# Router logits by token from the turned tile, twenty row homes, loops that skip an empty turn

## The chip, the core and the metric

The kernel runs on one core of a Trainium2 chip. The metric is device time in microseconds of one execution. The core has five engines that run their own instruction streams and meet at semaphores: TensorE (PE in the profile), VectorE (DVE), ScalarE (ACT), GpSimd (POOL) and SyncE (SP), which here only issues transfers. Before the change three runs took 599.23, 604.85 and 601.07 us, median 601.07.

## The reference, cut to what matters

There are 4 x 1024 = 4096 tokens of width H = 1024, a context of width D = 256, and E = 8 experts.

```python
def _L0_xattn_ref(x, adj, W, b):          # x is the context, adj the normed input
    si = jnp.einsum('bnd,d->bn', x, Wi[0])
    sj = jnp.einsum('bnd,d->bn', x, Wj[0])
    xij = jax.nn.sigmoid(si[:, :, None] + sj[:, None, :] + b[0])
    return P_ASEM * xij + (1.0 - P_ASEM) * adj

def _L0_ffn_ref(x, wg, W, b):
    xt = x.reshape(-1, Hv)
    logits = xt @ wg                       # 4096 x 8
    probs = jax.nn.softmax(logits, axis=-1)
    idx = jnp.argmax(probs, axis=-1)
    ...                                    # only the chosen expert's gate is kept
    expert_out = jnp.einsum('nh,eoh->neo', xt, W) + b[None, :, :]
    return jnp.einsum('ne,neo->no', combine, expert_out)

x = x + jnp.tanh(g_xattn[0]) * _L0_xattn_ref(ctx_512, _layernorm(x), ...)
x = x + jnp.tanh(g_ffn[0]) * _L0_ffn_ref(_layernorm(x), ...)
```

## The kernel before, in words

**First stage: 32 tiles of 128 tokens.** A tile is loaded into one of RX = 16 homes of the tile `xr` (SP, L366). DVE takes its statistics six tiles ahead (`stats`, L836), ACT computes the tanh form of the sigmoid three tiles ahead (`half_tanh`, L645), POOL applies the norm two tiles ahead (`linear`, L507), and DVE adds the two (`add_tanh`, L847). PE turns the tile with eight transposes (`turn_tile`, L1134), ACT copies the turned tile out of PSUM (`copy_turned`, L661), and PE multiplies it by the router weights `wg` (`route`, L1146). `route(t - 1)` stands behind `turn_tile(t)` in PE's stream. In `route` the eight columns of `wg` are loaded as weights and the 128 tokens of the turned tile stream, so the logits come out expert by token (8 x 128). In float32 each of the eight matmuls over k is two passes in the trace, 16 in all.

**By token.** For every group of four tiles ACT copies the logits out of PSUM (`logits_copy`, L668), and PE turns them with four small matmuls (`logits_by_token`, L1158). Then DVE picks the expert (`choose`, L857 and following), PE counts ranks (`rank`, L1167 to L1173), DVE makes positions (`position`, L885 and L887), and POOL scatters the finished rows into a table in memory (`store`, L515), sorted by expert. A home is free for the next load when its row is stored. SP issues its loads in order; the load of tile 19 stands behind `spread_scores(2)` and that of tile 26 behind `spread_scores(3)`, which wait for scores of the context.

**Context.** Eight groups of context are turned (L1108, eight transposes) and summed with two columns (`sum_columns`, L1124): there each 128 x 128 block is loaded as weights and two columns stream, 16 passes for a group. Groups 0 to 3 come ahead of tile 0, groups 4 to 7 behind tiles 2, 6, 10 and 14.

**Second stage: slots.** The sorted rows are worked in slots of 128 rows of one expert. A slot is 48 matmuls of 128 x 512 on PE (L1213, three products of high and low parts). DVE and ACT turn and split rows (L907, L679, L912) and, in two slots of each expert, four pieces of the next weights (L894, L673, L899). POOL makes the gate from the row's scalars (`slot_scalars`, L542 to L556), adds the scaled bias (L559, from ACT's L743) and stores the sums (`store_sums`, L563). DVE's `finish` (L924) adds the product and frees PE's PSUM pair: slot t + 2 of PE waits for `finish` of slot t.

**The loops.** The number of slots is known only at run time. There is room for SLOTS = 48, in loops of 6 slots to a turn (SP: 2). Two slots are worked ahead of the loop. The loops of PE, DVE, ACT and SP load a number from `slot_tab` for every slot, and branch around the slot if it is empty. POOL's loop looks at the first slot of a turn and leaves out the whole turn if that is empty.

Of the kernel before, what the change touches and what calls it, by code (L numbers as in the profile page):

```python
# [7 lines left out]
P = 128  # L8
# [13 lines left out]
def build(nc, x, ctx, g_xattn, g_ffn, mix_w, mix_b, wg, W, bias, out):  # L22
# [15 lines left out]
    RX = 16  # L38
# [36 lines left out]
    with st:  # L75
# [20 lines left out]
        wj_bc = sb("wj_bc", [P, DC, P])  # L96
# [48 lines left out]
        with zone:  # L145
            xr = [sb("xr0", [P, GR, ROW], F32, zone)]
            sb("even_weights", [P, 2, K, H], F32, zone)
            th = sb("th", [P, RTH, H], F32, zone)
            xr.append(sb("xr1", [P, RX - GR, ROW], F32, zone))
            ctx_in = sb("ctx_in", [P, 2, GR * D], F32, zone)  # L150
            ctx_tr = sb("ctx_tr", [P, GR, DC, P], F32, zone)
            sj = sb("sj", [P, 2, P, TB], F32, zone)
            xc_tr = sb("xc_tr", [P, 2, K, P], F32, zone)
            told = sb("told", [P, H], F32, zone)


# [15 lines left out]
        sb("gap", [P, 2 * K * H + RTH * H + (RX - GR) * ROW - 4 * K * H])  # L172
# [10 lines left out]
        early_ps = small[:, 128:129]  # L183
        tot_ps = pair[3][:, 0:E]

        lgt = bias_bc[0:E, 1, 0:HALF].rearrange("e (r n) -> e r n", r=GR)
# [43 lines left out]
        lgt_copied = sem("lgt_copied")  # L230
        by_token = sem("by_token")
# [46 lines left out]
        def rows_at(s, n):  # L278
            return xr[0][:, s:s + n, :] if s < GR else xr[1][:, s - GR:s - GR + n, :]
# [31 lines left out]
        def _(sp):  # L311
# [28 lines left out]
            for t in range(12, RX):  # L340
# [19 lines left out]
            for t in range(RX, T):  # L360
# [4 lines left out]
                sp.wait_ge(row_stored[slot_of(t)], 16)  # L365
# [15 lines left out]
            for s in range(RX):  # L381
                sp.wait_ge(row_stored[s], 16 * (T // RX))
# [15 lines left out]
            sp.wait_ge(by_token, NG)  # L398
# [3 lines left out]
            with sp.Fori(0, SLOTS // 2) as i:  # L402
                for r in range(2):
                    t = 2 * i + r + AHEAD
                    work = sp.value_load(slot_tab[0:1, 0, bass.ds(t, 1)], min_val=0, max_val=3)
                    with sp.If(work > 0):
                        sp.wait_ge(xb_turned, t + 2)
                        load_blocks(sp, sp.value_load(slot_tab[0:1, 2, bass.ds(t + 3, 1)], min_val=0,
                                                      max_val=E * N - P), r + 3)
                        with sp.If(work > 1):  # L410

                            n = sp.value_load(slot_tab[0:1, 3, bass.ds(t, 1)], min_val=2, max_val=HALVES - 1)
                            with sp.If(n < HALVES - 1):
                                n = sp.value_load(slot_tab[0:1, 3, bass.ds(t, 1)], min_val=2, max_val=HALVES - 2)
                                for m in range(WR):
                                    sp.wait_ge(w_turned, WR * n + m + 1)
                                    load_piece_of(n + 1, m)
                            with sp.Else():
                                sp.nop()
                            with sp.If(work < 3):  # L420

                                e = sp.value_load(slot_tab[0:1, 1, bass.ds(t, 1)], min_val=0, max_val=E - 2)
                                sp.wait_ge(w_ready, K * e + K + 1)
                                sp.dma_start(bias_bc[:, bass.ds((e + 1) % 2, 1), :].rearrange("p a h -> p (a h)"),
                                             bias[bass.ds(e + 1, 1), :].to_broadcast([P, H])).then_inc(bias_landed, 16)
                            with sp.Else():
                                sp.nop()
                            sp.nop()
                        with sp.Else():
                            sp.nop()  # L430
                        sp.nop()
                    with sp.Else():
                        sp.nop()

        @block.gpsimd
        def _(pool):
# [13 lines left out]
            nc.gpsimd.memset(xr[0][:, :, VAR + 1:LG], 0.0)  # L450
            nc.gpsimd.memset(xr[1][:, :, VAR + 1:LG], 0.0)
# [87 lines left out]
            def slot_scalars(u, n, k, k2):  # L539
# [17 lines left out]
                    gate_ready, 1)  # L557
                settled(rb_ready, u + 1)
# [10 lines left out]
            slot_scalars(0, 0, 0, 0)  # L569
            pool.wait_ge(limits_told, 1)  # L570
            slot_scalars(1, 0, 1, 1)
            store_sums(0, 0)
            slot_scalars(2, 1, 2, 0)
            store_sums(1, 1)
            pool.wait_ge(slots_told, 1)

            def slot(t, r, i):
# [3 lines left out]
                store_sums(t, r)  # L581

# [15 lines left out]
            held = [pool.value_load(in_place[0:1, s:s + 1], min_val=E, max_val=SLOTS) for s in range(2)]  # L598
            filled = pool.value_load(n_filled[0:1, 0:1], min_val=2 * E, max_val=SLOTS)
# [670 lines left out]
```

## Time and profile before

| what | value |
|---|---|
| median of three runs | 601.07 us |
| the profiled execution | 600.74 us, its span 599.0 us |
| mean granted TensorE clock | 0.949 of full |
| PE matmul busy | 545.9 us, 91% |
| DVE busy | 403.8 us, 67% |
| POOL busy | 332.5 us, 56% |
| ACT busy | 279.6 us, 47% |

Times in the profile count from the start of the span. The first stage runs from about 22 us (first `add_tanh`) to 161.6 us (last `route`), the second from there to the last sum at 585.6 us. The granted clock is a share of full speed: 1.00 is 2.4 GHz and 0.50 is 1.2 GHz. A busy time of PE says that matmuls were in flight, not that they went at full speed.

### The profile page before, as it was taken

To read this page: it belongs to the slowest core of one execution; us is meant where nothing else is said; L and a number is where in the kernel's file an instruction comes from. 1 tells how busy PE (TensorE), PEld (TensorE's weight loads), DVE (VectorE), ACT (ScalarE), POOL (GpSimd) and SP (SyncE) were. 2 spreads that over 40 slices of the span, in tenths; PEclk is the share of its full clock that TensorE was granted. 3 is DMA by queue.
4 is the path that set the end of the run, shared out by engine and by line. 5 is a ranking of instruction groups with operands and counts; after the bars stand their busy time and mean duration, and the time that the engine had idled before them with its cause. 6 is when DMAs were issued, how large, how long until landed. Compare 5 with 4: busy or idle time off the path is not lost.

```text
span 599.0 us, 13888 instructions
## 1 busy us (share of the span) xinstructions
PE 545.9 (91%) x2818; PEld 443.0 (74%) x2819; DVE 403.8 (67%) x534; ACT 279.6 (47%) x408; POOL 332.5 (56%) x500
## 2 busy tenths in 40 slices
PE   8899988898898969799989999998998999999990
PEld 6787766666677848688868888877887888888880
DVE  2867777796889876956955794784588559834320
ACT  4698868789513424424432442443244244332220
POOL 1788888888344443364356436435544663466650
PEclk9699889889899979989989999999999999999996
DMA  8997677887967987976875787688568757554530
GB/s 273 361 292 236 200 277 258 293 286 233 330 219 211 273 244 210 271 236 187 258 238 179 209 253 252 192 242 243 181 193 263 235 178 212 173 178 152 181 124 6
DMA packets 84398, 135.23 MB, mean 226 GB/s; under 512 B 12048, under 2 KB 64784, under 8 KB 84368
## 3 DMA queue, kind: packets, MB, share of 16 engines
q1 hardware_dynamic: 68432, 81.88, 46.9%
q0 software_dynamic: 9792, 33.82, 14.5%
q10 hardware_dynamic: 6144, 19.18, 10.3%
q8 instruction: 13, 0.21, 0.1%
q14 instruction: 17, 0.14, 0.1%
HBM read 101.01 MB, written 35.93 MB: 229 GB/s over the span
## 4 chain that ended last, share of the span: by engine, by line
PE 27%; DVE 22%; issue 15%; DMA 13%; POOL 8%; ACT 5%; ACTq 4%; DVEq 2%; POOLq 1%; SPq 0%
PE pair L1213 21%; DMA rows<-table 7%; DVE wt L899 7%; DVE pair L894 4%; DMA table<-xr,pos 3%; PE pair L1146 3%; DVE xt L912 2%; ACTq L747 2%; PE pair L1134 2%; DVE xr L847 2%; DVE raw L836 2%; DMA gates<-in_L_xattn_b 2%; DMA xr<-in_x 2%; POOL scal L552 1%; ACT wt L673 1%
## 5 line engine op out<-in xcount | busy, mean ns | idle before, releaser
L1213 PE MATMUL pair<-wt,xt 128*128 (+1 forms) x1728 | 401.9, 394 | 19.7 <-DVE rows L924 16.7
L1213 PEld LDWEIGHTS pair<-wt,xt 128*128 128x128 f32 x1728 | 328.1, 190 | 92.5 <-issue 22.4
L559 POOL TENSOR_TENSOR rows<-rows,rb 128x1024 f32<-128x1024 f32 x37 | 88.9, 2401 | 64.6 <-ACT rb L743 64.6
L673 ACT ACTIVATE wt<-pair 128x1024 f32 (+1 forms) x64 | 65.6, 1027 | 69.0 <-DVE pair L894 68.9
L912 DVE TENSOR_TENSOR xt<-pair,xt 128x1024 fp32r<-128x1024 f32 x38 | 46.5, 1224 | 70.6 <-ACT xt L679 70.6
L894 DVE STREAM_TRANSPOSE pair<-w_raw 128x1024 f32<-128x1024 f32 x64 | 79.8, 1249 | 1.4
L899 DVE TENSOR_TENSOR wt<-pair,wt 128x1024 f32 (+1 forms) x64 | 77.2, 1207 | 3.7 <-ACT wt L673 3.7
L743 ACT ACTIVATE rb<-bias_bc,scal 128x1024 f32 (+1 forms) x37 | 46.0, 1245 | 66.2 <-POOL scal L556 66.2
L1146 PE MATMUL pair<-xc_tr,wg_sb 128*8 128x128 f32 x512 | 70.2, 298 | 0.0
L552 POOL TENSOR_TENSOR scal<-scal,minus_one 128x1 f32<-128x1 f32 x37 | 20.4, 551 | 83.4 <-ACT ez L735 83.4
L679 ACT ACTIVATE xt<-pair 128x1024 fp32r<-128x1024 f32 x38 | 39.1, 1028 | 59.1 <-DVE pair L907 38.5
L924 DVE SCALAR_TENSOR_TENSOR rows<-pair,scal,rows 128x1024 f32<-128x1024 f32 x36 | 46.1, 1281 | 28.9 <-PE pair L1213 28.9
L907 DVE STREAM_TRANSPOSE pair<-xb 128x1024 f32<-128x1024 f32 x38 | 47.8, 1258 | 21.9 <-DMA xb<-table 17.1
L1146 PEld LDWEIGHTS pair<-xc_tr,wg_sb 128*8 128x8 f32 x512 | 47.1, 97 | 16.4 <-issue 2.8
L1134 PE MATMUL pair<-ident,xr 128*128 128x128 f32 x256 | 37.9, 295 | 14.9 <-DVE xr L847 14.9
L515 POOL DMA_INDIRECT table<-xr,pos x32 | 37.1, 1158 | 22.6 <-DVE pos L887 12.8
L836 DVE BATCH_NORM_STATS2 raw<-xr 128x6 f32<-128x512 f32 x64 | 40.7, 677 | 11.8 <-DMA xr<-in_x 11.8
L1134 PEld LDWEIGHTS pair<-ident,xr 128*128 128x128 f32 x256 | 30.4, 152 | 22.3 <-DVE xr L847 18.5
L507 POOL TENSOR_SCALAR xr<-xr,ln_a,ln_b 128x1024 f32<-128x1024 f32 x32 | 43.7, 1366 | 3.2
L563 POOL DMA_INDIRECT out_x<-rows,scatter_row x36 | 38.6, 1073 | 11.5 <-issue 6.6
L735 ACT ACTIVATE ez<-rows,scal 128x8 f32<-128x8 f32 x37 | 11.0, 296 | 72.3 <-POOL scal L547 72.3
L847 DVE SCALAR_TENSOR_TENSOR xr<-th,c,xr 128x1024 f32<-128x1024 f32 x32 | 41.5, 1297 | 4.1 <-POOL xr L507 3.8
(138 smaller groups left out, 378.7 us busy)
## 6 DMA issues: line engine op xcount, KB each, us to landing
w_raw<-in_L_ffn_W SPq DMA_DIRECT2D x256, 128.0 KB, 3.0
xb<-table SPq DMA_DIRECT2D x156, 128.0 KB, 3.2
rows<-table ACTq DMA_DIRECT2D x36, 520.0 KB
xr<-in_x SPq DMA_DIRECT2D x32, 512.0 KB, 6.0
ctx_in<-in_ctx SPq DMA_DIRECT2D x8, 512.0 KB, 7.8
bias_bc<-in_L_ffn_b SPq DMA_DIRECT2D x8, 512.0 KB, 4.4
sj<-sj_row SPq DMA_DIRECT2D x3, 512.0 KB, 5.1
rows<-table SPq DMA_DIRECT2D x2, 520.0 KB
```

The source lines that it names most:

```text
L559: nc.gpsimd.tensor_tensor(rows[:, k, 0:H], rows[:, k, 0:H], rb[:, :], ALU.add).then_inc(base_ready, 1)
L673: nc.scalar.activation(wt[:, bass.ds(place, 1), 0, :, P * m:P * (m + 1)].rearrange("p a k o -> p (a k) o"), ps[:, :].rearrange("p (k o) -> ...
L836: last = nc.vector.bn_stats(raw[:, t % 2, h, :], row_at(s)[:, HALF * h:HALF * (h + 1)])
L847: nc.vector.scalar_tensor_tensor(out=row_at(s)[:, 0:H], in0=th[:, t % RTH, :], scalar=c2[:, 0:1], in1=row_at(s)[:, 0:H], op0=ALU.mult, op1 ...
L894: nc.vector.transpose(turned(ps), blocked(w_raw[:, m, :, :])).then_inc(w_turned, 1)
L899: nc.vector.tensor_tensor(where[:, :, 1].rearrange("p a k o -> p (a k) o"), ps[:, :].rearrange("p (k o) -> p k o", k=K), where[:, :, 0].re ...
L907: nc.vector.transpose(turned(ps), blocked(xb[:, k, :, :])).then_inc(xb_turned, 1)
L912: nc.vector.tensor_tensor(where[:, :, 1].rearrange("p a k n -> p (a k n)"), ps[:, :], where[:, :, 0].rearrange("p a k n -> p (a k n)").bit ...
L924: nc.vector.scalar_tensor_tensor(out=row_of, in0=out_ps[r % 2][:, :], scalar=scal[:, bass.ds(k, 1), 7:8].rearrange("p a b -> p (a b)"), in ...
L1134: last = nc.tensor.transpose(xt_ps[t % 2][:, P * k:P * (k + 1)], row_at(slot_of(t))[:, P * k:P * (k + 1)], ident[:, :])
L1146: last = nc.tensor.matmul(lgt_ps[:, r, :], wg_sb[:, k, :], xc_tr[:, t % 2, k, :], start=(k == 0), stop=(k == K - 1))
L1213: last = nc.tensor.matmul(out_ps[r % 2][:, HALF * h:HALF * (h + 1)], xt[:, r % RING, x_part, k, :], wt[:, bass.ds(place + h, 1), w_part, k ...
```

## The change

1. **Router.** In `route` the turned tile is loaded as weights, 128 columns, and the eight columns of `wg` stream. The logits come out token by expert at once, so `logits_copy` on ACT and `logits_by_token` on PE are gone (8 of each), and `choose` waits for `route` alone. Logits and ranks have two homes in PSUM, by turns.
2. **Homes.** RX is 20. Four homes lie where the second weight half will be, so ACT waits for the rows of homes 16 to 19 to be stored before it writes piece (1, 0), at tile 28.
3. **Loops.** PE, DVE, ACT and SP leave a turn if its first slot is empty, as POOL does. POOL's three loads of end counts stand ahead of its loop.
4. **Orders.** In a slot POOL stores the sums of slot t before it adds the bias of slot t + 1, and ACT issues the load of the rows of slot t + 2 before the scaled bias of slot t + 1.

```diff
-    RX = 16
+    RX = 20
...
-            xr = [sb("xr0", [P, GR, ROW], F32, zone)]
-            sb("even_weights", [P, 2, K, H], F32, zone)
...
+            xr_late = sb("xr_late", [P, GR, ROW], F32, zone)
+            sb("first_half", [P, 2, K, HALF], F32, zone)
+            xr_last = sb("xr_last", [P, GR, ROW], F32, zone)
+            sb("second_half", [P, 2 * K * HALF - GR * ROW], F32, zone)
...
-            xr.append(sb("xr1", [P, RX - GR, ROW], F32, zone))
+            xr_first = sb("xr_first", [P, RX - 2 * GR, ROW], F32, zone)
...
-        lgt_ps, small = pair[3][0:E, 0:HALF].rearrange("e (r n) -> e r n", r=GR), pair[3][:, HALF:2 * HALF]
-        lg_ps = small[:, 0:GR * E].rearrange("p (r e) -> p r e", e=E)
-        rank_ps = small[:, 64:64 + GR * E].rearrange("p (r e) -> p r e", e=E)
...
+        lg_ps = [pair[3][:, HALF * j:HALF * j + GR * E].rearrange("p (r e) -> p r e", e=E) for j in range(2)]
+        rank_ps = [pair[3][:, HALF * j + 64:HALF * j + 64 + GR * E].rearrange("p (r e) -> p r e", e=E) for j in range(2)]
...
+            for t in range(12, 16):
...
+            for t in range(16, T):
                 if t == 19:
                     spread_scores(2)
                 if t == 26:
                     spread_scores(3)
-                sp.wait_ge(row_stored[slot_of(t)], 16)
+                if t >= RX:
+                    sp.wait_ge(row_stored[slot_of(t)], 16)
                 sp.dma_start(row_at(slot_of(t))[:, 0:H], tile_of(x_t, t)).then_inc(x_landed[slot_of(t)], 16)
...
-            sp.wait_ge(by_token, NG)
...
+            with sp.Fori(0, SLOTS // 2) as i:
+                t = 2 * i + AHEAD
+                first = work_of(t)
+                with sp.If(first > 0):
+                    slot(t, 0, first)
+                    second = work_of(t + 1)
+                    with sp.If(second > 0):
+                        slot(t + 1, 1, second)
...
+            def add_base(u, k):
                 settled(rb_ready, u + 1)
                 nc.gpsimd.tensor_tensor(rows[:, k, 0:H], rows[:, k, 0:H], rb[:, :], ALU.add).then_inc(base_ready, 1)
...
+            held = [pool.value_load(in_place[0:1, s:s + 1], min_val=E, max_val=SLOTS) for s in range(2)]
+            filled = pool.value_load(n_filled[0:1, 0:1], min_val=2 * E, max_val=SLOTS)
...
             def slot(t, r, i):
                 slot_scalars(t + 1, RING * i + (r + 1) // 2, (r + 1) % RING, (r + 1) % 2)
                 settled(out_stored[r % 2], 16 * RING * i + 16 * (r // 2))
                 store_sums(t, r)
+                add_base(t + 1, (r + 1) % RING)
...
-            held = [pool.value_load(in_place[0:1, s:s + 1], min_val=E, max_val=SLOTS) for s in range(2)]
-            filled = pool.value_load(n_filled[0:1, 0:1], min_val=2 * E, max_val=SLOTS)
...
-            def logits_copy(g):
-                act.wait_ge(routed, GR * (g + 1))
-                if g:
-                    act.wait_ge(by_token, g)
-                nc.scalar.activation(lgt, lgt_ps, ACT.Copy).then_inc(lgt_copied, 1)
...
-                if r == 1 and g > 0:
-                    logits_copy(g - 1)
...
+                    if PIECE_AT[t] == (1, 0):
+                        for s in range(RX - GR, RX):
+                            act.wait_ge(row_stored[s], stores_from(s))
...
+            def slot(t, r, i, work):
+                behind = (r + 2) % RING
+                settled(summed, t + 1)
+                xt_high(t + 2, behind, cut_a)
+                with act.If(work > 1):
+                    n = table_of(3, t, HALVES - 1)
+                    home = act.snap(n % 4)
+                    for m in range(WR):
+                        cut_high(n, m, home, (cut_b, cut_a)[m % 2])
+                with act.Else():
+                    act.nop()
+                after = (r + 1) % RING
+                exp_sum(t + 1, after)
+                settled(out_stored[(r - 1) % 2], 16 * RING * i + 16 * ((r - 1) // 2) + 16)
+                load_rows(act, table_of(2, t + 2, E * N - P), r, behind)
+                e1 = table_of(1, t + 1, E - 1)
+                scaled_bias(t + 1, after, e1, act.snap(e1 % 2))
             with act.Fori(0, SLOTS // TURN) as i:
...
                 g, r = t // GR, t % GR
                 if t == 0:
                     pe.wait_ge(ctx_copied, GR)
-                if r == 0 and g > 0:
-                    pe.wait_ge(lgt_copied, g)
+                    pe.wait_ge(sj_col_ready, 2)
+                    pe.wait_ge(si_ready, GR)
+                if r == 0 and g > 1:
+                    pe.wait_ge(pos_ready, g - 1)
                 for k in range(K):
-                    last = nc.tensor.matmul(lgt_ps[:, r, :], wg_sb[:, k, :], xc_tr[:, t % 2, k, :],
+                    last = nc.tensor.matmul(lg_ps[g % 2][:, r, :], xc_tr[:, t % 2, k, :], wg_sb[:, k, :],
                                             start=(k == 0), stop=(k == K - 1))
                 last.then_inc(routed, 1)
...
-            def logits_by_token(g):
-                pe.wait_ge(lgt_copied, g + 1)
-                if g:
-                    pe.wait_ge(pos_ready, g)
-                else:
-                    pe.wait_ge(sj_col_ready, 2)
-                    pe.wait_ge(si_ready, GR)
-                for r in range(GR):
-                    last = nc.tensor.matmul(lg_ps[:, r, :], lgt[:, r, :], ident[0:E, 0:E], start=True, stop=True)
-                last.then_inc(by_token, 1)
...
                     pe.wait_ge(ahead_told, 1)
-                nc.tensor.matmul(rank_ps, ones_bf[:, :],
+                nc.tensor.matmul(rank_ps[g % 2], ones_bf[:, :],
...
-                if r == 1 and g > 0:
-                    logits_by_token(g - 1)
                 if r == 2 and g > 0:
                     rank(g - 1)
...
             with pe.Fori(0, SLOTS // TURN) as i:
-                for r in range(AHEAD, TURN + AHEAD):
-                    t = TURN * i + r
-                    work = pe.value_load(slot_tab[0:1, 0, bass.ds(t, 1)], min_val=0, max_val=3)
-                    with pe.If(work > 0):
-                        e = pe.value_load(slot_tab[0:1, 1, bass.ds(t, 1)], min_val=0, max_val=E - 1)
-                        multiply(t, r, e, pe.snap(2 * (e % 2)))
-                    with pe.Else():
-                        pe.nop()
+                with pe.If(work_of(TURN * i + AHEAD) > 0):
+                    slot(TURN * i + AHEAD, AHEAD)
+                    for r in range(AHEAD + 1, TURN + AHEAD):
+                        with pe.If(work_of(TURN * i + r) > 0):
+                            slot(TURN * i + r, r)
```

PE's stream at tiles 4 to 6 of the first stage, before (`xc_tr` is the turned tile, `wg_sb` the router weights, `bias_bc` the copied logits; names on the right of the arrow are what is read):

```order
L1134 MATMUL pair<-ident,xr 128x128 x8
L1158 MATMUL pair<-ident,bias_bc 128x8 x4
L1146 MATMUL pair<-xc_tr,wg_sb 8x128 x8
L1134 MATMUL pair<-ident,xr 128x128 x8
L1167 MATMUL pair<-cum,ones_bf 128x32
L1170 MATMUL pair<-onehot,ones_bf 128x24
L1170 MATMUL pair<-onehot,ones_bf 128x16
L1170 MATMUL pair<-onehot,ones_bf 128x8
L1173 MATMUL pair<-onehot,lower_bf 128x32
L1146 MATMUL pair<-xc_tr,wg_sb 8x128 x8
```

And of the change, at the same place:

```order
L1163 MATMUL pair<-ident,xr_first 128x128 x8
L1177 MATMUL pair<-wg_sb,xc_tr 128x8 x8
L1163 MATMUL pair<-ident,xr_first 128x128 x8
L1187 MATMUL pair<-cum,ones_bf 128x32
L1190 MATMUL pair<-onehot,ones_bf 128x24
L1190 MATMUL pair<-onehot,ones_bf 128x16
L1190 MATMUL pair<-onehot,ones_bf 128x8
L1193 MATMUL pair<-onehot,lower_bf 128x32
L1177 MATMUL pair<-wg_sb,xc_tr 128x8 x8
```

The four small matmuls are gone, and each router matmul gives 128 x 8 instead of 8 x 128: 8 columns stream where 128 did.

ACT's stream at the end of a slot in the loop, before (`ez` is the row's exponentials, `rb` the scaled bias):

```order
L735 ACTIVATE ez<-rows,scal 128x8
...
L743 ACTIVATE rb<-bias_bc,scal 128x1024
L611 ISA
L747 ISA
L747 TENSOR_LOAD slot_tab
L747 ISA x2
L307 ISA
L307 DMA rows<-table 128x1040
```

And of the change:

```order
L312 DMA rows<-table 128x1040
L761 ISA
L761 TENSOR_LOAD slot_tab
L761 ISA x2
L631 ISA
L757 ISA
L757 ACTIVATE rb<-bias_bc,scal 128x1024
L814 UNCONDITIONAL_BRANCH
```

The load of rows stood behind the scaled bias and now stands ahead of it.

## Rows read from the trace of the kernel before

**Rows 1.** The profile's page, its head and its row of granted clock, 40 slices.

```profile
span 599.0 us, 13888 instructions
...
PEclk9699889889899979989989999999999999999996
```

**Rows 2.** Busy time by stretch: length, each engine's busy time, clock, DMA share, GB/s.

```profile
22.00:157.00 135.00, 119.14 (x919) 92.96 (x918) 102.14 (x197) 108.93 (x179) 112.29 (x131) 0.89 0.80 267
217.00:584.00 367.00, 355.76 (x1536) 291.93 (x1534) 237.50 (x227) 135.28 (x180) 186.96 (x298) 0.98 0.69 211
```

**Rows 3.** Groups by line: busy us, mean ns, then idle before.

```profile
L1146 PE MATMUL pair<-xc_tr,wg_sb 128*8 128x128 f32 x512 | 70.2, 298 | 0.0
...
L1158 PE MATMUL pair<-ident,bias_bc 8*128 8x8 f32 x64 | 8.4, 254 | 1.0 <-ACT bias_bc L668 1.0
```

**Rows 4.** Timeline of PE, first stage: start, length, line, shape, count, idle before.

```profile
30.63 1.09 PE L1134 MATMUL pair<-ident,xr 128*128 128x128 f32 x8
31.65 1.91 PE L1146 MATMUL pair<-xc_tr,wg_sb 128*8 128x128 f32 x16
...
59.82 3.40 PE L1146 MATMUL pair<-xc_tr,wg_sb 128*8 128x128 f32 x16
...
152.12 1.97 PE L1134 MATMUL pair<-ident,xr 128*128 128x128 f32 x8 [1.33 <-DVE xr L847]
```

**Rows 5.** Timeline of PE from 13 to 22 us, the context ahead of tile 0.

```profile
13.42 1.93 PE L1124 MATMUL pair<-wcol,xc_tr 128*128 128x2 f32 x16
15.21 3.23 PE L1108 MATMUL pair<-ident,ctx_in 128*128 128x128 f32 x16
18.24 2.25 PE L1124 MATMUL pair<-wcol,ctx_tr 128*128 128x2 f32 x16
20.35 1.93 PE L1124 MATMUL pair<-wcol,xc_tr 128*128 128x2 f32 x16
```

**Rows 6.** PE by stretch: length, busy, granted clock, DMA share, GB/s.

```profile
16.00:18.00 2.00, 2.00 (x11) 0.50 1.02 399
20.00:22.00 2.00, 2.00 (x20) 1.00 1.00 401
22.00:24.00 2.00, 0.46 (x4) 0.62 1.01 414
```

**Rows 7.** Waits of DVE from 22 to 157 us: total, times, longest.

```profile
DVE top L857 <- PE pair L1158: 12.2, 5, 3.9
DVE raw L836 <- DMA xr<-in_x: 11.6, 4, 4.8
```

**Rows 8.** Waits over the whole span: total, times, longest.

```profile
PE pair L1213 <- DVE rows L924: 16.7, 6, 5.6
...
ACT xt L679 <- issue: 19.1, 16, 1.5
```

**Rows 9.** Timeline from 224 to 255 us, slots with weights.

```profile
224.98 1.24 ACT L743 ACTIVATE rb<-bias_bc,scal 128x1024 f32 x1 [1.82 <-POOL scal L556]
225.90 0.34 ACTq L307 DMA_DIRECT2D rows<-table  x1
227.35 1.03 ACT L679 ACTIVATE xt<-pair 128x1024 fp32r<-128x1024 f32 x1 [1.12 <-issue]
228.41 1.23 DVE L912 TENSOR_TENSOR xt<-pair,xt 128x1024 fp32r<-128x1024 f32 x1 [4.04 <-ACT xt L679]
...
254.93 5.35 PE L1213 MATMUL pair<-wt,xt 128*128 x16 [3.04 <-DVE rows L924]
```

**Rows 10.** Timeline of the end: the last sum and the last store.

```profile
584.33 1.28 DVE L924 SCALAR_TENSOR_TENSOR rows<-pair,scal,rows 128x1024 f32<-128x1024 f32 x1 [5.97 <-PE pair L1213]
...
586.51 1.07 POOL L563 DMA_INDIRECT out_x<-rows,scatter_row  x1 [2.44 <-DVE rows L924]
```

**Rows 11.** SP's waits, its last one in the span.

```profile
SPq L75 <- PEq L75: 15.0, 1, 15.0
```

**Rows 12.** DMA issues of the stores: count, median us to landing.

```profile
out_x<-rows,scatter_row POOLq DMA_INDIRECT x36, 4.3
```

More of the change, by code:

```diff
@@ L787, in _ @@
+            with act.Fori(0, SLOTS // TURN) as i:
+                first = table_of(0, TURN * i + AHEAD, 3)
+                with act.If(first > 0):
+                    slot(TURN * i + AHEAD, AHEAD, i, first)
+                    for r in range(AHEAD + 1, TURN + AHEAD):
+                        work = table_of(0, TURN * i + r, 3)
+                        with act.If(work > 0):
+                            slot(TURN * i + r, r, i, work)
                         with act.Else():
                             act.nop()
-                        after = (r + 1) % RING
@@ new lines, in slot @@
+            def slot(t, r, i, work):
+                behind, mine = (r + 2) % RING, r % RING
+                dve.wait_ge(xt_ready, t + 2)
+                turn_rows(t + 2, RING * i + r // 2 + 1, r % 2, cut_a)
+                with dve.If(work > 1):
+                    n = dve.value_load(slot_tab[0:1, 3, bass.ds(t, 1)], min_val=0, max_val=HALVES - 1)
+                    home = dve.snap(n % 4)
+                    for m in range(WR):
+                        turn_weights(n, m, (cut_b, cut_a)[m % 2])
+                        if m == 0:
+                            xt_low(t + 2, behind, cut_a)
+                            dve.wait_ge(xt_ready, t + 3)
+                        else:
+                            cut_low(n, m - 1, home, (cut_b, cut_a)[(m - 1) % 2])
+                    cut_low(n, WR - 1, home, cut_a)
+                    settled(w_ready, WR * n + WR)
+                with dve.Else():
+                    xt_low(t + 2, behind, cut_a)
+                finish(t, r, mine)
@@ new lines, in work_of @@
+            def work_of(t):
+                return dve.value_load(slot_tab[0:1, 0, bass.ds(t, 1)], min_val=0, max_val=3)
+            with dve.Fori(0, SLOTS // TURN) as i:
+                first = work_of(TURN * i + AHEAD)
+                with dve.If(first > 0):
+                    slot(TURN * i + AHEAD, AHEAD, i, first)
+                    for r in range(AHEAD + 1, TURN + AHEAD):
+                        work = work_of(TURN * i + r)
+                        with dve.If(work > 0):
+                            slot(TURN * i + r, r, i, work)
@@ L1084, in _ @@
                         with dve.Else():
-                            xt_low(t + 2, behind, cut_a)
-                        finish(t, r, mine)
-                    with dve.Else():
-                        dve.nop()
+                            dve.nop()
+                    dve.nop()
+                with dve.Else():
+                    dve.nop()
         @block.tensor
```

151 lines of the change are left out of this document (62 added, 89 removed).

## The prediction

> **What bounds the kernel now.** I began with the head of the page: a span of 599.0 us, and a row of granted clock that stands at 9 or 8 in most slices of the second half and dips to 7 in the first [rows 1]. The profiled execution took 600.74 us, so 1.7 us lie outside its span, and it is 0.3 below the median of 601.07; the sum below starts from 600.7. The busy time by stretch [rows 2] gives two stages with different limits. In the second stage, 217 to 584 us, PE is in flight for 355.8 of 367.0 us and its clock is 0.98: the stage is the matmuls plus the gaps between them. In the first, 22 to 157 us, no engine is full, but four are near it: PE 119.1 of 135.0 us, POOL 112.3, ACT 108.9, DVE 102.1, at a mean clock of 0.89. With 32 tiles from about 24 us to 161.6 us this is 4.3 us for a tile. Last I read the waits: DVE waits 12.2 us for the logits by token and 11.6 us for rows of x [rows 7], and PE waits 16.7 us for `finish` of two slots before, six times [rows 8].
>
> **The router, in columns.** Now 512 router passes take 70.2 us of PE and the 64 small passes 8.4 us [rows 3]. At full clock one tile is a turn of 1.09 us and a route of 1.91 us [rows 4]. Sixteen passes in which 128 x 128 blocks are the weights and two columns stream, the sums of the context, take 1.93 us at full clock [rows 5]. So to stream 8 columns in place of 128 gives nothing directly: the weight load sets the pace of such a pass, 1.91 against 1.93. What goes is the small matmuls, 8 x 1.05 us on PE, and eight copies of the logits on ACT.
>
> **The router, in clock.** This is where I expect the change to decide. Ahead of tile 0 PE does the same kind of work that the new `route` does, and the granted clock tells what it does to it. After the sums at 13.42 us the clock is 0.50 from 16 to 18 us, with PE in flight for 2.00 of 2.00 us [rows 6]; the transposes at 15.21 us, 128 streaming columns each, run at this level, 3.23 us for 16 [rows 5]. After them it is 1.00 from 20 to 22 us. The two groups of sums at 18.24 and 20.35 us follow without a break, and from 22 us it is 0.62, that is, it falls to 0.50 in the stretch [rows 6]. So passes with few streaming columns do not hold 2.4 GHz, however closely they stand, and passes with 128 columns bring it back. In the first stage today the route streams 128 columns in two thirds of PE's passes. After the change those have 8, and only the turn, 8 of 24 passes of a tile, streams 128.
>
> The Trainium skill ("TensorE: Matmul & The Clock Gate", Part 1, What's actually happening) says that activity releases the throttle and idle time restores it. If being in flight were that activity, the clock would stay up, and the time would be that of rival B; the trace speaks against it with 0.50 at 2.00 of 2.00 us.
>
> At the low clock a turn is 1.97 us and a route 3.40 us [rows 4]. The route of 3.40 us is the old form; I take the same for the new one, since both forms agree at full clock. A tile is then 1.97 + 3.40 less 0.15 for the overlap of the groups (31.72 against 31.65 us at full clock, twice that at the low one), 5.2 us. That is more than the 4.3 us of today, so PE becomes the bound of the stage, and neither DVE's waits nor POOL matter in it. The sum: 32 x 5.2 = 166.4 us; four groups of context behind tiles 2, 6, 10 and 14, each a turn and a set of 16 sums, 4 x 5.3 = 21.2 us; ranks some 2 us. From 24 us this ends at 213.6 us. Against it stand spells of high clock: where the 8 transposes of a context group stand beside the 8 of a turn there are 16 in a row, as at 15.21 us, and the spell that followed there began in the sums at 18.24 us and was over early in 22 to 24 us: a bit over 3 us in which PE does twice the work. Not each of the four will line up so well; I take three, worth 10 us. The last route then ends at 203.6 us instead of 161.6: **+42 us**. Bounds: +52 with no spell; +13 if the clock is low in only half of the tiles (16 x 5.2 + 16 x 4.3 + 8 for the sums of context at low clock = 160, from 24 to 184, less 10).
>
> The same skill page (Part 4, PE-mode transpose) says that a transpose does not count as PE being busy in the same way, so that full clock is not granted for it. By this there would be no spells, the stage would be longer, and the time that of rival D. The trace disagrees: the clock rose behind the 16 transposes of 15.21 us. It saw this once, though, and with matmuls of two columns ahead and behind.
>
> **The homes.** Rows of x come too late by 11.6 us in four waits [rows 7], as SP waits for the store of the tile 16 before. With 20 homes they go, though the load of tile 19 still stands behind the scores of the context. ACT's new wait at tile 28 for homes 16 to 19 finds stores of many tiles before; I cost it at nothing. The cover of all of it is PE's pace: a tile every 5.2 us leaves DVE, POOL and ACT idle for about 1 us or more of each. So the homes are worth 0 here, and only in rival B anything.
>
> **The orders in a slot.** In slots with weights DVE waits up to 4.04 us for ACT's high part at L679 [rows 9]. ACT is late since its load of rows stands behind the scaled bias, which waits for POOL's gate (1.82 us) and takes 1.24 us; after the load ACT needs another 1.12 us before L679. DVE's `finish` is then late, and PE stands still, 3.04 us at 254.93 us, and its next slot runs partly at 0.50. Six such waits sum to 16.7 us, the longest 5.6 [rows 8]. The longest stands in the prologue at 216 us, where DVE has the backlog of the first weights; the orders do not reach it. The other five are 11.1 us, and after the three long ones the clock is low for some us, at about 1.5 us each: 15 us at stake. The new order issues the load 1.2 us sooner, and the bias stands later by the load. POOL's store leaves 1.1 us sooner and its bias 1.1 us later, which delays `finish` of the next slot only if DVE is then early. I take two thirds less a little for that: **-11 us**, bounds -15 and -4.
>
> **The empty turns.** 36 stores are issued [rows 12], so of 48 slots 12 are empty; two are worked ahead, so the loop's 48 places end two beyond the last slot, and 14 places are an empty check today. With the change four are left: two in the sixth turn and one each for the last two turns. The last sum ends at 585.6 us and the last store is issued at 586.51 us with 1.07 us [rows 10]; from there to 599.0 us nothing is done but checks and the wait of SP for PE, 15.0 us [rows 11]. ACT spends 19.1 us on 16 gaps of issue [rows 8], 1.2 us each, which is what one such load and branch costs. PE's check is of the same kind, so ten fewer are up to 12 us of its end. But the store must land (4.3 us, [rows 12]), and what closes the program on other engines is not in any row. I take **-4 us**, bounds -7 and -1.
>
> **Sum:** 600.7 + 42 - 11 - 4 = 627.7, forecast **628 us**, own range 604 to 645: from +25 (part of the stage spared) with the best of the other terms to +52 with -7 and 0.
>
> **Rivals.**
> B, the clock holds and the kernel is faster. The turns alone, 8 passes of 128 columns in each tile, would have to hold 2.4 GHz as 24 do now. Then PE needs 3.0 us for a tile and the 8.4 us go; DVE's waits of 12.2 and 11.6 us go too, but POOL has 112.3 us of work in 135 and is often without a break, so I take only a third of them, -7 (bounds -12 and -2). 600.7 - 7 - 11 - 4 = 579, 568 to 588. For it: PE has slack in each tile, and its transposes come early. Against it: rows 6, twice. It decides from the point where the mean clock of the stage stays above about 0.8, for then a tile of PE is below 4.3 us. Chance 0.14.
> D, no spells, since PE's few columns outweigh the transposes even beside the context: 600.7 + 52 - 11 - 4 = 638. Chance 0.12; its time lies in the same range.
> C, low clock in half of the stage, with fuller use of the high half: 600.7 + 13 - 11 - 4 = 599, 594 to 606. Turns pack closer in places, once PE lags and works back to back. Chance 0.06.
> E, the orders give nothing, because `finish` waits for the later bias, and the router is as forecast: 600.7 + 42 + 0 - 3 = 640. Chance 0.08.
> The forecast itself has 0.60.
>
> **Range and chances.** 598 to 645 takes in the forecast, D, E and half of C, and leaves out B, half of C and the outer edge of the forecast, 0.2. What can be told from no change is 1%, 6 us. Faster: B, with a piece of C, 0.15. Within 1%: C and the low edge, 0.07. Slower: 0.78.
>
> **What would show it.** In the profile after, the granted clock from 24 to 160 us: about 0.55 to 0.65 if right, 0.8 or more in rival B. The groups of router passes: 3.4 us for a tile in most, against 1.9. The end of the last `route`: near 204 us, against 155 in B. PE in flight for nearly all of the stage, with DVE's waits for raw rows and logits gone or turned into waits for PE. In the second stage: PE's waits for `finish` at L924 down from six to one or two, and ACT's L679 without 4 us of DVE waiting. At the end: SP's last wait some 5 to 10 us shorter. The forecast is wrong if the turns hold the clock by themselves, or if a pass with 8 columns is quicker than 3.4 / 16 us at the low clock.

## The result and the profile after

The changed kernel takes 624.7 us (median of four runs, 622.3 to 629.0) against 602.1 us for the kernel before in the same comparison: 1.038 times as long, 95% interval 1.030 to 1.047. The forecast was 628 us, range 598 to 645. The profiled execution took 622.37 us and its span is 620.7 us, so 1.7 us lie outside the span, as before.

The page, its granted clock in 40 slices, one for 15.5 us:

```profile
span 620.7 us, 13529 instructions
...
PEclk9575555655555989799999999999999999999996
```

From the second slice to the end of the first stage (twelve slices) ten stand at 5, one at 6 and one at 7, where [rows 1] had 8 and 9 in the stage behind a 6 in its first slice. The second stage is nearly as it was.

Busy time by stretch, for the same two stretches as [rows 2] (length, then PE, PE's weight loads, DVE, ACT, POOL, and last clock, DMA share, GB/s):

```profile
22.00:157.00 135.00, 134.88 (x720) 134.11 (x721) 83.91 (x164) 86.58 (x144) 86.86 (x110) 0.55 0.63 222
...
217.00:584.00 367.00, 357.79 (x1556) 294.53 (x1555) 263.38 (x253) 143.81 (x191) 188.26 (x304) 0.99 0.76 226
```

PE is in flight for 134.9 of 135.0 us, with fewer matmuls (720, 919 before), at a mean clock of 0.55. POOL went from 112.3 to 86.9 us and ACT from 108.9 to 86.6: they wait. PE is the bound of the first stage. The router group of the page answers to [rows 3]:

```profile
L1177 PE MATMUL pair<-wg_sb,xc_tr 128*128 128x8 f32 x512 | 102.9, 339 | 0.0
```

The same 512 passes took 70.2 us. PE's timeline around the first context group among the tiles, and one that comes later (start, length, line, shape, count), shows both levels of the clock:

```profile
25.47 4.04 PE L1163 MATMUL pair<-ident,xr_first 128*128 128x128 f32 x16
29.29 3.42 PE L1177 MATMUL pair<-wg_sb,xc_tr 128*128 128x8 f32 x16
...
34.31 3.42 PE L1177 MATMUL pair<-wg_sb,xc_tr 128*128 128x8 f32 x16
37.58 1.95 PE L1137 MATMUL pair<-ident,ctx_in 128*128 128x128 f32 x8
39.32 1.53 PE L1163 MATMUL pair<-ident,xr_first 128*128 128x128 f32 x8
40.69 1.85 PE L1177 MATMUL pair<-wg_sb,xc_tr 128*128 128x8 f32 x16
...
46.80 1.62 PE L1163 MATMUL pair<-ident,xr_first 128*128 128x128 f32 x8
48.21 3.42 PE L1177 MATMUL pair<-wg_sb,xc_tr 128*128 128x8 f32 x16
...
79.19 1.95 PE L1137 MATMUL pair<-ident,ctx_in 128*128 128x128 f32 x8
80.93 1.92 PE L1163 MATMUL pair<-ident,xr_first 128*128 128x128 f32 x8
...
190.12 6.83 PE L1177 MATMUL pair<-wg_sb,xc_tr 128*128 128x8 f32 x32
```

A route is 3.42 us at the low clock and 1.85 at the full one. The clock rises inside the turn at 39.32 us, behind eight transposes of context and among those of the turn, and is down again inside the turn at 46.80, 6.8 us later. Sixteen transposes in a row do not always raise it: behind those of 25.47 us and those of 79.19 and 80.93 us it stays at 0.50. The other two context groups, at 56.82 and 104.68 us, have a spell of some 3.4 us each. From 29.29 to 34.31 us is one tile: 5.02 us. The last route ends at 196.95 us (161.7 before).

In the second stage, waits over the whole span, for [rows 8]:

```profile
DVE xt L934 <- ACT xt L693: 40.4, 23, 3.4
...
PE pair L1231 <- DVE rows L946: 6.9, 3, 4.2
```

PE waits 6.9 us for `finish`, three times, against 16.7 us in six. DVE's wait for ACT's high part is 40.4 us, and 70.6 before. The end, for [rows 10]:

```profile
607.50 1.28 DVE L946 SCALAR_TENSOR_TENSOR rows<-pair,scal,rows 128x1024 f32<-128x1024 f32 x1 [4.73 <-PE pair L1231]
609.70 1.07 POOL L579 DMA_INDIRECT out_x<-rows,scatter_row  x1 [4.14 <-DVE rows L946]
610.81 2.35 POOL L575 TENSOR_TENSOR rows<-rows,rb 128x1024 f32<-128x1024 f32 x1
```

These rows tell when each engine's stream reaches the line that closes the program (L75; `DRAIN` is its step there, of 8, 17 or 5628 ns; `POOLq` is POOL's stream, `PEldq` PE's, and the two times are both its start), first before:

```profile
L75 POOLq DRAIN  x1: 5628/5628/5628, 593.2 to 593.2; - x1
L75 ACTq DRAIN  x1: 8/8/8, 593.6 to 593.6; - x1
L75 PEldq DRAIN  x1: 8/8/8, 595.6 to 595.6; - x1
L75 DVEq DRAIN  x1: 17/17/17, 598.6 to 598.6; - x1
```

and changed:

```profile
L75 PEldq DRAIN  x1: 8/8/8, 608.8 to 608.8; - x1
L75 ACTq DRAIN  x1: 8/8/8, 610.5 to 610.5; - x1
L75 DVEq DRAIN  x1: 17/17/17, 612.8 to 612.8; - x1
...
L75 POOLq DRAIN  x1: 5628/5628/5628, 614.8 to 614.8; - x1
```

Counted from the last sum, PE is there at once and not 10 us later, DVE after 4 us and not 13. POOL, whose step takes 5.63 us in both, begins it 6.0 us after the last sum and not 7.6: it ends last in both.

The 21.7 us between the spans divide, by the end of the last route and of the last sum:

| profiled execution | first stage ends | then to last sum | then to end of span |
|---|---|---|---|
| before | 161.7 | 423.9 | 13.4 |
| changed | 196.95 (+35.2) | 411.8 (-12.1) | 11.9 (-1.5) |

Forecast were +42, -11 and -4.

### The profile page after: what moved, and what is told of

It is laid out like the page before. It is cut to its first block, busy times and chain, and to the rows that moved or that the text cites. A ratio compares the mean times of both kernels' runs of the same rounds, so it can differ in the third digit from the quotient of the medians.

```text
span 620.7 us, 13529 instructions
## 1 busy us (share of the span) xinstructions
PE 594.4 (96%) x2754; PEld 518.9 (84%) x2755; DVE 404.8 (65%) x534; ACT 276.0 (44%) x400; POOL 325.9 (53%) x501
## 4 chain that ended last, share of the span: by engine, by line
PE 72%; DVE 11%; issue 5%; DMA 4%; POOL 1%; ACT 1%; ACTq 1%; DVEq 1%; POOLq 0%; SPq 0%
PE pair L1231 45%; PE pair L1177 16%; PE pair L1163 8%; DVE wt L921 4%; DVE pair L916 2%; PE pair L1153 2%; DMA out_x<-rows,scatter_row 2%; DMA gates<-in_L_xattn_b 2%; DVE rows L946 1%; PE pair L1137 1%; ACT wt L687 1%; DVE xt L934 1%; DVE raw L858 1%; DMA xb<-table 1%; ACTq L761 1%
## 5 line engine op out<-in xcount | busy, mean ns | idle before, releaser
L1177 PEld LDWEIGHTS pair<-wg_sb,xc_tr 128*128 128x128 f32 x512 | 104.6, 311 | 0.1
L1177 PE MATMUL pair<-wg_sb,xc_tr 128*128 128x8 f32 x512 | 102.9, 339 | 0.0
L934 DVE TENSOR_TENSOR xt<-pair,xt 128x1024 fp32r<-128x1024 f32 x38 | 46.5, 1225 | 41.6 <-ACT xt L693 40.4
L681 ACT ACTIVATE xc_tr<-pair 128x1024 f32<-128x1024 f32 x32 | 32.7, 1023 | 56.3 <-PE pair L1163 56.3
L1163 PE MATMUL pair<-ident,xr_first 128*128 128x128 f32 x192 | 44.2, 407 | 0.1
L529 POOL DMA_INDIRECT table<-xr_first,pos x24 | 29.5, 1228 | 26.3 <-DVE pos L909 19.4
L1163 PEld LDWEIGHTS pair<-ident,xr_first 128*128 128x128 f32 x192 | 39.6, 233 | 0.5 <-DVE xr_first L869 0.5
L665 ACT ACTIVATE th<-sj,si_half 128x1024 f32<-128x1024 f32 x32 | 36.5, 1142 | 0.1
L869 DVE SCALAR_TENSOR_TENSOR xr_first<-th,c,xr_first 128x1024 f32<-128x1024 f32 x24 | 30.9, 1288 | 4.4 <-POOL xr_first L521 4.1
```

Of the source, the lines that this page charges most:

```text
L934: nc.vector.tensor_tensor(where[:, :, 1].rearrange("p a k n -> p (a k n)"), ps[:, :], where[:, :, 0].rearrange("p a k n -> p (a k n)").bit ...
L1163: last = nc.tensor.transpose(xt_ps[t % 2][:, P * k:P * (k + 1)], row_at(slot_of(t))[:, P * k:P * (k + 1)], ident[:, :])
L1177: last = nc.tensor.matmul(lg_ps[g % 2][:, r, :], xc_tr[:, t % 2, k, :], wg_sb[:, k, :], start=(k == 0), stop=(k == K - 1))
```

## The experiments

The kernel before ran beside each; its median was 602.0 us in the first comparison, 601.5 in the second and 601.0 in the third.

**How many columns stream (wide128).** This is the changed kernel, with the same stationary operand and the same order. Only the eight columns of `wg` are streamed sixteen times over:

```diff
-                    last = nc.tensor.matmul(lg_ps[g % 2][:, r, :], xc_tr[:, t % 2, k, :], wg_sb[:, k, :],
+                    last = nc.tensor.matmul(pair[3][:, HALF * (g % 2) + E * r:HALF * (g % 2) + E * r + 128].rearrange("p (c e) -> p c e", e=E),
+                                            xc_tr[:, t % 2, k, :], wg_sb[:, k, :].unsqueeze(1).to_broadcast([P, 16, E]),
                                             start=(k == 0), stop=(k == K - 1))
```

(The columns that are too many are written over by the next tile of the group; the ranks' home in PSUM moves from column 64 to 272.)

> The changed kernel, but the router's matmuls stream the eight columns of wg sixteen times over (128 columns) through the same turned tile as weights; the logits are the first eight of each. Theory 'few streaming columns lower the clock': the granted clock from 22 to 157 us is back at 0.85 to 0.95 (changed kernel 0.55), a route takes 1.9 us, the last route ends at 150 to 160 us (196.8), and the time is 600.7 - 7 (homes, 0 to 12) - 12 (second stage) - 1.5 (end) = about 580 us, 575 to 588. Rival 'it is the weight side: a fresh 128-column weight for each pass, or the order of PE's stream': the clock stays at 0.55 and the time at 620 to 629 us.

Measured: 586.4 us, 0.975 of before, interval 0.971 to 0.980. Its busy time in the first stage, and its router group over the span:

```profile
22.00:157.00 135.00, 110.71 (x898) 106.77 (x899) 105.92 (x199) 108.26 (x177) 117.17 (x132) 0.92 0.77 261
```

```profile
L1177 PE MATMUL pair<-wg_sb,xc_tr 128*128 128x128 f32 x512 | 66.9, 286 | 0.0
```

The clock is 0.92, PE has slack again (110.7 us), and the last route ends at 159.4 us. With sixteen times the columns and the same weight loads the kernel is 38 us quicker. This shows that the streaming columns, by way of the clock, made the loss; it was not the weight side, the order of the stream or the missing copy.

**The old router with all else changed (oldroute).** `route`, `logits_copy` and `logits_by_token` as before:

```diff
-                    last = nc.tensor.matmul(lg_ps[g % 2][:, r, :], xc_tr[:, t % 2, k, :], wg_sb[:, k, :],
+                    last = nc.tensor.matmul(lgt_ps[:, r, :], wg_sb[:, k, :], xc_tr[:, t % 2, k, :],
...
+                if r == 1 and g > 0:
+                    logits_by_token(g - 1)
```

> The changed kernel with the old router (expert by token, copy on ACT, four small matmuls), homes, loops and orders as changed. Theory 'the router cost all of the loss, the orders gave the gain of the second stage': clock of the first stage 0.87 to 0.92, last route at 150 to 161 us, from there to the last sum 412 us as in the changed kernel (424 before), time 580 to 588 us. Rival 'the second stage was shorter because the slow first stage let VectorE and ScalarE catch up with their weights': from the last route to the last sum 420 to 425 us, time 592 to 599 us.

Measured: 588.2 us, 0.978 (0.975 to 0.981). The last route ends at 162.9 us, and from there to the last sum it is 411.2 us. The clock of the first stage is 0.94. Last route, clock and time are each a little past what was expected. The second stage keeps its gain though the first is quick again, so the slow first stage did not buy it. Against wide128 the small matmuls and copies cost about 1.8 us, less than the noise of a run.

**The new router alone (newroute).** The kernel before with change 1 only:

```diff
-                    last = nc.tensor.matmul(lgt_ps[:, r, :], wg_sb[:, k, :], xc_tr[:, t % 2, k, :],
+                    last = nc.tensor.matmul(lg_ps[g % 2][:, r, :], xc_tr[:, t % 2, k, :], wg_sb[:, k, :],
...
-                if r == 1 and g > 0:
-                    logits_by_token(g - 1)
```

> The kernel before with the new router alone (16 homes, old loops, old orders). Theory 'the router cost all of the loss': clock of the first stage 0.55, last route at 195 to 199 us, from there to the last sum 422 to 426 us, time 600.7 + 35 = 636 us, 631 to 641. Rival 'the slow first stage shortens the second by itself': from the last route to the last sum 412 to 415 us, time 622 to 627 us.

Measured: 641.6 us, 1.065 (1.059 to 1.071), a little past the upper end that was expected. Last route at 202.2 us, from there 424.3 us to the last sum. Its first stage has the changed kernel's picture at a clock of 0.53. It ends 5 us later, and the clock rose beside two context groups only, about 40 and 88 us, for some 3 us each, which is about 7 us less at full clock than in the changed kernel. VectorE waits for no row of x there, with 16 homes. The row:

```profile
22.00:157.00 135.00, 132.79 (x680) 131.96 (x681) 78.95 (x157) 83.11 (x137) 84.30 (x106) 0.53 0.63 207
```

**Half and a quarter of the columns (wide64, wide32).** As wide128, with 64 and 32 in place of 128 (the columns of `wg` eight times and four times over; the written part of PSUM is as wide):

```diff
-                                            xc_tr[:, t % 2, k, :], wg_sb[:, k, :].unsqueeze(1).to_broadcast([P, 16, E]),
+                                            xc_tr[:, t % 2, k, :], wg_sb[:, k, :].unsqueeze(1).to_broadcast([P, 8, E]),
```

> As the changed kernel, but 64 columns stream in a router pass (the eight of wg, eight times), half of what streamed before. Theory 'the clock follows how many columns stream': between the changed kernel (8 columns, clock 0.55, 624.7 us) and 128 columns (0.92, 586.4 us). By equal steps from 8 to 128 columns 64 lie near the middle: clock 0.70 to 0.88, last route at 165 to 185 us, time 593 to 612 us. Rival 'only full passes count': clock 0.55 to 0.60, 618 us or more. Rival 'half is as good as all': clock 0.90 or more, 590 us or less.

> As the changed kernel, but 32 columns stream in a router pass. Theory 'the clock follows how many columns stream': clock 0.58 to 0.72, time 605 to 621 us. Rival 'below some number nothing changes': clock 0.53 to 0.57, 622 to 629 us.

Measured: 593.2 us (0.987, 0.981 to 0.993) with 64 and 620.9 us (1.029, 1.022 to 1.036) with 32. Here are three parts of the first stage of the kernel with 64 columns:

```profile
22.00:60.00 38.00, 35.58 (x241) 35.06 (x240) 28.43 (x50) 28.84 (x49) 29.68 (x36) 0.70 0.80 246
...
60.00:90.00 30.00, 30.00 (x189) 29.88 (x189) 18.22 (x42) 22.16 (x39) 21.00 (x30) 0.64 0.90 325
...
90.00:157.00 67.00, 60.89 (x412) 59.79 (x412) 53.47 (x101) 52.99 (x84) 55.77 (x62) 0.75 0.64 212
```

With 64 the clock changes level often, 0.71 over the stage, and the last route ends at 167.2 us, near the quick end of what was expected: a mean clock of 0.71 is nearly enough, since PE had slack at 0.92. With 32 it is 0.55 and the first stage ends at 196.5 us, as with 8. Whether 32 columns are a little quicker than 8 stays open: the medians are 620.9 and 624.7 us and the intervals of the ratios overlap, but no run with 32 took as long as the fastest with 8. For 32 the rival "nothing changes" has the profile on its side and the theory the time, which lies in its range; for 64 the theory holds in both.

**Both orders (orders), ACT's alone (act_order), POOL's alone (pool_order).** All on the kernel before.

```diff
 POOL, a slot
                 store_sums(t, r)
+                add_base(t + 1, (r + 1) % RING)
 ACT, a slot
-                        e1 = table_of(1, t + 1, E - 1)
-                        scaled_bias(t + 1, after, e1, act.snap(e1 % 2))
                         settled(out_stored[(r - 1) % 2], 16 * RING * i + 16 * ((r - 1) // 2) + 16)
                         load_rows(act, table_of(2, t + 2, E * N - P), r, behind)
+                        e1 = table_of(1, t + 1, E - 1)
+                        scaled_bias(t + 1, after, e1, act.snap(e1 % 2))
```

> The kernel before with the two orders of a slot alone (POOL stores the sums before it adds the next bias, ACT loads rows before the scaled bias). Theory 'the orders give the second stage its gain': PE's waits for the sum of two slots before fall from 16.7 to under 8 us, last route as before at 161 us, time 588 to 592 us. Rival 'they give nothing by themselves': 599 to 603 us, PE's waits stay at 14 us or more.

> The kernel before with ACT's order alone: the load of rows ahead of the scaled bias. Theory 'ACT's load was what held its high part, and by it the sum of a slot and PE': all of the gain of both orders, from the last route to the last sum 410 to 413 us (423.9 before), time 588 to 593 us. Rival 'half is POOL's, whose store frees the rows that ACT's load waits for': 416 to 420 us, time 594 to 598 us.

> The kernel before with POOL's order alone: the store of the sums ahead of the next bias. Theory 'ACT's load is all of it': from the last route to the last sum 422 to 425 us, time 600 to 604 us, and the end no shorter. Rival 'half is POOL's': 416 to 420 us, time 594 to 598 us.

Measured: both 592.2 us (0.985, 0.982 to 0.988). ACT's alone 611.8 us (1.015, 1.011 to 1.020), POOL's alone 609.3 us (1.014, 1.008 to 1.019): each by itself makes the kernel slower, which no theory had expected. From the last route to the last sum they take 434.3 and 427.5 us (423.9 before); with POOL's alone another 3.7 us stand in the first stage of the profiled execution, which the edit does not touch. The waits from 217 to 584 us tell part of why. First both orders:

```profile
POOL out_x L565 <- DVE rows L929: 55.2, 19, 4.2
...
DVE xt L917 <- ACT xt L685: 41.8, 25, 3.7
...
ACT rb L749 <- issue: 8.5, 3, 3.4
...
PE pair L1218 <- DVE rows L929: 7.3, 3, 4.0
```

ACT's order alone:

```profile
POOL rows L559 <- ACT rb L743: 87.7, 32, 5.1
DVE xt L911 <- ACT xt L679: 81.3, 26, 5.4
...
ACT rb L743 <- issue: 65.8, 19, 5.1
...
PE pair L1212 <- DVE rows L923: 22.8, 9, 4.0
```

POOL's order alone:

```profile
DVE xt L918 <- ACT xt L685: 86.0, 26, 6.5
...
POOL scal L542 <- DMA rows<-table: 52.1, 29, 3.3
POOL out_x L565 <- DVE rows L930: 33.7, 13, 2.6
...
PE pair L1219 <- DVE rows L930: 18.0, 7, 5.6
```

ACT's load of the rows of slot t + 2 waits until the store of slot t - 1 has landed. With ACT's order alone that store still stands behind POOL's bias, and the scaled bias now stands behind the load. So ACT's scaled bias is held in its queue for 65.8 us where it was held by nothing of the kind before, POOL waits 87.7 us for it (59.7 before), its store goes later still, and PE waits 22.8 us. With POOL's order alone the store may go early, but ACT issues the load no sooner, and POOL's gate waits 52.1 us for rows (24.9 before). It is not that the later base holds ACT's one home of `rb`: ACT's scaled bias waits for POOL's gate as before (59.1 us, 59.4 before) and for nothing else. The waits for `finish`, 18.0 us, are hardly more than the 16.7 of before, while PE's weight loads at this line stand 20.9 us (14.0 before) with nothing in the profile that ends the wait. So what makes this version slow is only in part shown. With both, store and load move ahead together: PE's waits fall to 7.3 us, and the stage from 423.9 to 410.2 us in the profiled execution.

**Loops and homes alone (loops_homes).** The kernel before with changes 2 and 3 only, made as oldroute with both orders turned back:

```diff
 POOL, a slot
+                add_base(t + 1, (r + 1) % RING)
                 settled(out_stored[r % 2], 16 * RING * i + 16 * (r // 2))
                 store_sums(t, r)
-                add_base(t + 1, (r + 1) % RING)
 ACT, a slot
+                e1 = table_of(1, t + 1, E - 1)
+                scaled_bias(t + 1, after, e1, act.snap(e1 % 2))
                 settled(out_stored[(r - 1) % 2], 16 * RING * i + 16 * ((r - 1) // 2) + 16)
                 load_rows(act, table_of(2, t + 2, E * N - P), r, behind)
-                e1 = table_of(1, t + 1, E - 1)
-                scaled_bias(t + 1, after, e1, act.snap(e1 % 2))
```

> The kernel before with the changed loops and the twenty homes alone (old router, old orders). The end, from the last sum to the end of the span, is 13.4 us before and 11.9 us changed. Theory 'the exits are worth the 4 us that were forecast, but the new order puts a bias of 2.35 us behind the last store, on POOL's way to the end': the end is 9 to 10 us here, from the last route to the last sum 423 to 426 us, time 596 to 600 us. Rival 'the exits are worth 1.5 us by themselves': the end is 11.7 to 12.2 us, time 598 to 602 us.

Measured: 595.5 us, 0.991 (0.988 to 0.995). Last route at 163.3 us, last sum at 582.4, end of the span 594.1:

```profile
span 594.1 us, 13680 instructions
```

```profile
581.11 1.28 DVE L961 SCALAR_TENSOR_TENSOR rows<-pair,scal,rows 128x1024 f32<-128x1024 f32 x1 [5.98 <-PE pair L1257]
```

The end is 11.7 us, 1.7 less than before, and the theory that the bias behind the last store had hidden the rest fell. Nor would the exits give the 1.7 us by themselves: POOL's stream ends last here too (its 5.63 us begin at 588.3 us, 5.9 behind the last sum), and what is gone from it are the three loads of end counts, which now stand ahead of its loop. Before they took POOL from 590.8 to 592.4 us:

```profile
L598 POOLq TENSOR_LOAD <-in_place x2: 288/292/295, 590.8 to 591.4; - x2
...
L599 POOLq TENSOR_LOAD <-n_filled x1: 286/286/286, 591.9 to 591.9; - x1
```

The time is lower than both expectations: the second stage is 419.1 us, 4.8 less than before, and PE's waits for `finish` are four and 12.8 us. No run separates the loops from the homes in this.

**The homes (wide128_b, wide128_late).** The second holds SP's loads back as if there were 16 homes:

```diff
+                sp.wait_ge(row_stored[slot_of(t - 16)], 16)
                 if t >= RX:
                     sp.wait_ge(row_stored[slot_of(t)], 16)
```

> The changed kernel with 128 streaming router columns again, as the partner of the next run: 584 to 588 us.

> As its partner, but SP's load of the row of tile t also waits for the store of tile t - 16, as if there were 16 homes. Theory 'POOL's work bounds the first stage and the homes give at most a few us': VectorE's waits for rows of x are 6 to 12 us again, last route 0 to 3 us later, time within 3 us of the partner. Rival 'the homes are what made the first stage short': last route 5 to 10 us later, 592 us or more.

Measured: 586.1 and 586.2 us, both 0.975 of before. With the loads held back DVE waits again from 22 to 157 us:

```profile
DVE raw L859 <- DMA xr_last<-in_x: 9.4, 4, 7.0
DVE raw L859 <- DMA xr_first<-in_x: 8.8, 4, 4.2
```

These are 18.2 us of waiting, more than was expected, and they cost nothing that the medians show. The last route ends at 164.7 us in its profiled execution and at 160.5 in its partner's, a little more than the 0 to 3 us later that were expected, but single executions of one first stage differ by as much: it ends at 161.7 us in the kernel before and at 165.4 with POOL's order alone.

## Why the prediction was right

**The clock** carried it. The step was that passes with few streaming columns do not hold 2.4 GHz however closely they stand, read from [rows 5] and [rows 6], around the context's sums. One of its two witnesses was weak: in the stretch from 22 us PE was in flight for only 0.46 of 2.00 us, so idle time could have lowered the clock as well. The changed kernel shows it with PE in flight throughout, and wide128 shows that it is the cause. The Trainium skill ("TensorE: Matmul & The Clock Gate", Part 1) ties the clock to how busy PE is; this kernel is in flight for 134.88 of 135.00 us at 0.55, so being in flight was not enough to hold it up. Part 4 of this page of the Trainium skill says that a transpose does not count as busy in the same way; here the clock rose at 39 to 41 us, behind and among 16 transposes with nothing else of many columns near, as it had behind those of 15.21 us before. Rival D is out by that, though two other sets of 16 raised nothing.

**The direct cost** of a pass was right at both levels: 3.42 us for a route at the low clock (3.40 taken), 1.85 at the full one (1.91).

**The size of the first stage** was 7 us too high, +42 against +35.2. The mis-sized term is the tile: I took the overlap of 0.15 us once, but it is there at both joins, turn to route and route to turn, so that a tile is 5.02 us instead of 5.2. 32 of these are 5.8 us. The spells came as forecast in kind: three of them, beside the context groups, the first twice as long as I took, some 13 us at full clock in place of 10. The first turn stood at 25.47 us and not at 24, which takes 1.5 us back. That it was three is in part luck: newroute, with the same router, had two.

**The orders** were mis-sized by little, -12.1 us in the second stage against -11, and -9.8 us in the medians of the two orders alone. Not all of the -12.1 need be theirs, since loops_homes has -4.8 without them. And the account behind it was incomplete. I had put the gain to ACT's earlier load and counted POOL's earlier store as a by-effect; the runs show that neither gives anything without the other. A forecast for either alone would have had the wrong sign.

**The empty turns** had the wrong path: -4 taken, -1.5 measured, -1.7 with loops and homes alone. I priced ten checks at up to 1.2 us each and took a third of it. The exits did bring PE's stream to its end 10 us sooner after the last sum, and DVE's 9 us. But POOL ends last, before and after, and it had left its empty turns already; what it does sooner is its three loads of end counts. Behind these stand 5.63 us of its closing step, which the change does not touch. I had written that what closes the program on other engines is in no row; the trace has it, in the rows of L75. Before, DVE ended 0.2 us ahead of POOL, so without the exits DVE would probably have held back most of what POOL gained: the 1.5 us need both. SP's last wait did not shrink by 5 to 10 us, as I had taken for a sign: it grew from 15.0 to 19.8 us, since SP's stream now comes to its end 7.9 us ahead of the last sum and not 1.6.

**The homes** were costed at nothing and gave nothing that a run shows, even where the clock is high and PE does not hide them.

**Rival B** would have been close in kind, too fast in size: with the clock held the kernel takes 586.4 us, not 579. Its first stage ends at 159.4 us, 2.3 less than before, where I had granted 7 for DVE's waits; POOL, 117.2 us in 135, keeps the pace.

The measured 624.7 us is 3.3 below the forecast: 7 less in the first stage and 1 less in the second, 2.5 more at the end, the rest the distance of the profiled execution from the median. Errors of both signs stand in it, so that it came so near is in part luck. The upper end of my own range, 645, took -7 and 0 for the other two terms, where their bounds of -4 and -1 give 648; nothing hung on it.

The fastest two versions are the new router with 128 streaming columns, 586.4 and 586.1 us, and the old router with the other changes, 588.2 us. Both orders alone (592.2), 64 columns (593.2) and loops and homes alone (595.5) also beat both kernels.

## What to carry to other kernels

Before turning a matmul around so that fewer columns stream, look for rows in the same trace where so few stream, and read the granted clock beside them: two passes of equal length at full clock can leave the clock at different levels, and at the low one a pass takes nearly twice as long (a route 3.42 us against 1.85). If it falls, streaming the same columns many times over can bring it back, and at full clock it cost a route 0.1 us here (1.95 us against 1.85). Before pricing the end of a program, look which engine's stream closes last; work taken from the others gives nothing by itself. And where two engines wait for each other through a transfer, price their orders together: one of two moves can have the opposite sign of the pair.

## What I had not expected

- More streaming made a kernel 38 us quicker with the same weight loads (624.7 to 586.4 us).
- With 64 columns in the router the clock did not settle at a level in the stage: 0.70, 0.64 and 0.75 in three parts of it, while with 32 it was 0.55 over the stage.
- At the low clock a route takes nearly the same with 8, 32 or 128 streaming columns: 32 passes took 6.83 us with 8 (190.12 us above) and 6.88 us with 32 in its own trace, and 16 took 3.40 us with 128 in the old form [rows 4].
